# GpSimd takes over the high halves of the FFN weights, and three of the FFN's waits move

## The reference

```
def _tlin(x, w, s):                       # w holds -1, 0 and 1
    return jnp.einsum('bsi,oi->bso', x, w) * s
h = jax.nn.silu(_tlin(x, w1_w, w1_s)) * _tlin(x, w2_w, w2_s)      # 512 -> 2048
h = jax.nn.gelu(_tlin(h, h1_w, h1_s), approximate=False)          # 2048 -> 2048
h = jax.nn.gelu(_tlin(h, h2_w, h2_s), approximate=False)          # 2048 -> 2048
return _tlin(h, w3_w, w3_s)                                       # 2048 -> 512
...
x = x + jnp.tanh(g_xattn[0]) * _L0_xattn_ref(_layernorm(x), ctx_1024, ...)
x = x + jnp.tanh(g_ffn[0]) * _L0_ffn_ref(_layernorm(x), ...)      # this one
x = x + jnp.tanh(g_xattn[1]) * _L1_xattn_ref(_layernorm(x), ctx_1024, ...)
x = x + jnp.tanh(g_ffn[1]) * _L1_ffn_ref(_layernorm(x), ...)
```

## Time and profile before

| | before |
|---|---|
| median of 3 runs (1685.14 to 1689.29) | 1686.5 us |
| the profiled execution, its own time | 1688.01 us |
| its span in the trace | 1686.2 us |
| PE busy | 1601.1 us, 95% of the span |
| DVE, ACT, POOL busy | 1100.2, 966.3, 290.8 us |
| FFN of layer 0 (first to last start of L995) | 520.4 to 1074.1 us |

### The profile page before, as it was taken

How to read it: one execution, slowest core, us unless ns; L and a number is a source line. 1 busy time by engine, 2 the same in 40 slices (tenths; PEclk the granted TensorE clock), 3 DMA queues, 4 the chain that set the end, 5 groups by cost and what they waited for, 6 DMA issues and landing times.

```text
span 1686.2 us, 25732 instructions
## 1 busy us (share of the span) xinstructions
PE 1601.1 (95%) x9298; PEld 1448.8 (86%) x9298; DVE 1100.2 (65%) x1949; ACT 966.3 (57%) x2014; POOL 290.8 (17%) x407
## 2 busy tenths in 40 slices
PE   5899999999988999999899989989999999999898
PEld 5788999899977999999899986777999989998655
DVE  5367877787786673333655545546777777778786
ACT  4367776777664454343544444236767667776575
POOL 2022121212142000000100000002111111113641
PEclk9999999999999999999999999999999999999899
DMA  6567776776562225554255625354766577657400
GB/s 191 129 157 180 189 180 167 179 190 178 144 179 78 90 89 185 189 175 170 94 197 203 215 98 169 106 122 122 194 169 178 151 186 183 167 137 191 155 12 28
DMA packets 146232, 257.74 MB, mean 153 GB/s; under 512 B 40916, under 2 KB 90196, under 8 KB 145968
## 3 DMA queue, kind: packets, MB, share of 16 engines
q1 hardware_dynamic: 145648, 255.79, 54.1%
q10 hardware_dynamic: 448, 0.14, 0.0%
HBM read 187.46 MB, written 58.57 MB: 146 GB/s over the span
## 4 chain that ended last, share of the span: by engine, by line
PE 82%; DVE 6%; issue 5%; ACT 4%; DMA 1%; POOL 1%; ACTq 0%; SPq 0%; DVEq 0%; POOLq 0%
PE ps L995 26%; PE ps L684 16%; PE ps L680 14%; PE ps L731 7%; PE ps L743 7%; PE ps L801 2%; PE ps L718 2%; PE ps L721 2%; PE ps L936 2%; PE ps L949 1%; ACT P L1654 1%; DVE wl_f L1546 1%; PE ps L859 1%; PE ps L720 1%; PE ps L719 1%
## 5 line engine op out<-in xcount | busy, mean ns | idle before, releaser
L995 PE MATMUL ps<-ah_f,wh_f 128*128 128x400 f32 (+1 forms) x1296 | 446.5, 346 | 9.3 <-DVE al_f L1559 5.6
L995 PE MATMUL ps<-al_f,wh_f 128*128 128x400 f32 (+1 forms) x1296 | 444.7, 344 | 0.0
L995 PEld LDWEIGHTS ps<-ah_f,wh_f 128*128 128x128 f32 x1296 | 245.4, 189 | 12.5 <-issue 10.7
L995 PEld LDWEIGHTS ps<-al_f,wh_f 128*128 128x128 f32 x1296 | 245.7, 190 | 0.0
L1154 DVE TENSOR_REDUCE nmax<-ps 100x1 f32<-100x722 f32 x256 | 220.6, 903 | 38.3 <-PE ps L720 34.7
L1654 ACT ACTIVATE P<-ps,nmax 100x722 f32<-100x722 f32 x256 | 220.2, 862 | 32.2 <-DVE nmax L1154 32.1
L1983 POOL TENSOR_TENSOR cxl<-raw,cxh 128x384 fp32r<-128x384 f32 (+1 forms) x120 | 118.9, 1013 | 659.9 <-ACT cxh L1619 653.0
L1663 ACT ACTIVATE PT<-ps 128x400 fp32r<-128x400 f32 x384 | 166.9, 505 | 80.1 <-PE ps L731 78.9
L1160 DVE TENSOR_TENSOR PT<-ps,PT 128x400 fp32r<-128x400 f32 x384 | 196.7, 566 | 3.6
L680 PE MATMUL ps<-cxh,wkh 128*128 128x338 f32 (+1 forms) x512 | 174.7, 341 | 22.9 <-DVE wkl L1133 13.3
L1542 DVE CAST wh_f<-raw_f 128x1024 fp32r<-128x1024 f32 x85 | 58.8, 691 | 184.8 <-PE ps L995 160.5
(11 more groups left out here) (191 smaller groups left out, 2614.9 us busy)
## 6 DMA issues: line engine op xcount, KB each, us to landing
KS<-kd SPq DMA_DIRECT2D x192, 361.0 KB
raw_f<-in_h SPq DMA_DIRECT2D x64, 512.0 KB, 5.0
raw_f<-in_gud SPq DMA_DIRECT2D x48, 512.0 KB, 5.8
raw<-in_ctx SPq DMA_DIRECT2D x64, 192.0 KB, 3.6
kd<-ksh SPq DMA_DIRECT2D x64, 192.0 KB, 2.1
kd<-ksl SPq DMA_DIRECT2D x64, 192.0 KB, 2.4
raw_f<-in_w SPq DMA_DIRECT2D x24, 512.0 KB, 3.8
raw<-in_ctx SPq DMA_DIRECT2D x64, 169.0 KB, 4.5
```

The costliest lines, as they stand in the source:

```text
L995: return e.matmul(o, p, q, start=start, stop=stop)
```

## The change

GpSimd casts unit u's high half (`high_unit`, new semaphore g_wh), for units 3 to 87. DVE keeps the subtraction, which now waits for g_wh, and makes it at the start of step u instead of its end; ACT's measure moves to the start of its step too. Steps 47 and 79 (`LATE`) keep both at the end. PE waits for g_wh ahead of a unit, and for g_low only at the load of the register. Unit 16 takes k = 4 to 7 before 0 to 3. The products of unit 80 begin after 62 Gelus instead of 64 and wait for 64 at batch 6, whose bank the last Gelu reads.

```diff
+LATE = (47, 79)
...
             def high(z, jobs):
                 for j in jobs:
+                    if j[3] and j[2][1] == 6 * S:
+                        w.wait_ge(a_gelu, 64)
                     one((wh, act[0]), z, j, j[4], False)
...
                 if u < 3:
                     w.wait_ge(g_ul, u + 1)
                 else:
-                    w.wait_ge(v_ul, u - 2)
+                    w.wait_ge(g_wh, u - 2)
+                for k, jobs in groups[:-1]:
+                    input_ready(u, k)
+                    high(z, jobs)
+                input_ready(u, groups[-1][0])
                 if u < 3:
                     w.wait_ge(v_low, 1)
                 else:
                     w.wait_ge(g_low, u - 2)
-                for k, jobs in groups[:-1]:
-                    input_ready(u, k)
-                    high(z, jobs)
-                input_ready(u, groups[-1][0])
                 e.reg_load(reg, low[0:1, z, 1:2].bitcast(I32))
...
+                order = [4, 5, 6, 7, 0, 1, 2, 3] if u == 16 else range(8)
...
-            w.wait_ge(a_gelu, 64)
+            w.wait_ge(a_gelu, 62)
...
-            def prepare(u):
+            def low_unit(u):
+
                 z, r = u % 4, FETCHED["unit", u] % 4
-                w.wait_ge(d_raw[r], raw_done(("unit", u)))
+                w.wait_ge(g_wh, u - 2)
                 if u >= 4:
                     w.wait_ge(p_u, u - 3)
-                me.then(e.tensor_copy(wh[:, z, :], raw[:, r, :]))
-                me.settle()
-                if u >= 4:
                     w.wait_ge(a_raw, FREE_AT["unit", u - 4] + 1)
...
             for u in range(UNITS):
+                if u + 3 < UNITS and u not in LATE:
+                    low_unit(u + 3)
...
-                if u + 3 < UNITS:
-                    prepare(u + 3)
+                if u in LATE:
+                    low_unit(u + 3)
...
             for u in range(UNITS):
+                if u + 3 < UNITS and u not in LATE:
+                    measure_low(u + 3)
...
-                if u + 3 < UNITS:
+                if u in LATE:
                     measure_low(u + 3)
...
+            def high_unit(u):
+
+                z, r = u % 4, FETCHED["unit", u] % 4
+                w.wait_ge(d_raw[r], raw_done(("unit", u)))
+                if u >= 4:
+                    w.wait_ge(p_u, u - 3)
+                e.tensor_copy(wh[:, z, :], raw[:, r, :]).then_inc(g_wh, 1)
+
             attention(0)
+            high_unit(3)
             for u in range(UNITS):
+                if 4 <= u + 1 < UNITS:
+                    high_unit(u + 1)
                 if u >= 3:
                     spread_low(u)
```

More of the change, by code:

```diff
@@ L281, in flamingo_kernel @@
         g_ones, g_cx, g_ql, g_rx, g_low, g_tot = (sem("g_" + n) for n in ("ones", "cx", "ql", "rx", "low", "tot"))
-        g_xf, g_ul = (sem("g_" + n) for n in ("xf", "ul"))
+        g_xf, g_ul, g_wh = (sem("g_" + n) for n in ("xf", "ul", "wh"))
         g_self, g_nh, g_xr, g_wo, g_ol, g_rq, g_xn, g_xq = (
@@ L1058, in _ @@
                         w.wait_ge(a_gelu, 32 * layer + 2 * (n - 4) + 2)
+                order = [4, 5, 6, 7, 0, 1, 2, 3] if u == 16 else range(8)
                 products(u, [(8 * q + kk, [(ps[:, p + half, 0:HN], (128 * kk, 128 * kk + 128),
                                             (8 * q + kk, HN * half, HN * half + HN), False,
-                                            q == 0 and kk == 0, q == 1 and kk == 7) for half in range(2)])
-                             for kk in range(8)]).then_inc(p_u, 1)
-            w.wait_ge(a_gelu, 64)
+                                            q == 0 and i == 0, q == 1 and i == 7) for half in range(2)])
+                             for i, kk in enumerate(order)]).then_inc(p_u, 1)
+            w.wait_ge(a_gelu, 62)
             for u in range(80, 88):
```

## The result

The changed kernel takes 1660.7 us, median of four runs (1659.97 to 1663.37), against 1685.8 for the kernel before on the same chip: a ratio of 0.985 with a 95% interval of 0.983 to 0.987. The time is 1.5% lower, and the interval lies clear of 1. The forecast was 1663.0, faster, with a range of 1660 to 1670. The profiled execution took 1663.37 us (span 1661.6) against 1688.01 (span 1686.2).

The account below looks back on a forecast made before the run. PE, busy 95% of the span, was taken to bound the kernel, losing time at three layer boundaries. Gains 3.6 + 10.2 + 9.4 + 0.3 = 23.5 us from 1688.0 give 1664.5, less 1.5 for the median: 1663.0, range 1660 to 1670.

Parts of the forecast that it names:

- three boundaries: Layer boundaries 15/16, 47/48 and 79/80 in the FFN, where PE stands still and the clock falls behind it.
- Unit 16: Boundary 15/16: starting with k = 4 to 7 covers DVE's late splits; 7.2 us instead of 10.78, gain 3.6.
- Boundary 47/48: Unit 49's measure and subtraction ahead of the copies: units 49 and 50 without waits, 11.66 us instead of 21.86, gain 10.2.
- GpSimd waits out DVE's streams: Shared memory: GpSimd's casts yield to DVE's back-to-back work; if one came between two splits, unit 49 would lose 0.8 us.
- Unit 80: Boundary 79/80: starting after 62 Gelus leaves no wait; 7.37 us instead of 16.81, gain 9.4.
- The first wait: Start of the FFN: PE's wait on v_low moves behind 12 matmuls, gain 0.3 us.
- Casts on GpSimd cost nothing: Every step: 85 casts of 1.04 us join the all-reduces, 1.4 us in every 5.83, hidden by PE's products.
- The reload: GpSimd's library reload at the start, behind unit 4's cast: margin 0.7 us; costs nothing at 6.96 us, 2.1 at 9.76.
- the late all-reduce: Rival at unit 50: all-reduce late behind unit 51's cast, most of the 10.2 us lost, 1673; chance 4%.
- the wait at the register load: Rival: the wait keeps PE from running ahead, up to 0.5 us in each of 88 units, 1707; chance 4%.
- a reload in each unit: Rival: GpSimd reloads its library between cast and all-reduce, some 215 us slower, 1880; chance 2%.
- given back in part: Rival: long reload (2.1), cast inside the splits (0.8), clock falling at unit 16 (1.5); together 4.4 us, 1667.4; chance 13%.

Follow-up runs that it names:

- experiment 10: The kernel before, unchanged, run again for a second trace: 1685.9 us, ratio 1.000.
- experiment 8: Changed kernel with GpSimd's first cast held, unit 16 in order 4, 5, 6, 0, 1, 2, 3, 7, and unit 51's cast held past the splits: 1660.5 us.
- Experiments 4 and 6: First: kernel before with only unit 80's early start, 1683.1 us. Second: changed kernel without exceptions at steps 47 and 79 (LATE empty), 1676.9 us.
- experiment 7: Changed kernel with PE's wait for g_low back at the head of a unit: 1666.5 us, ratio 0.989.
- experiment 12: Changed kernel with every cast of a high half made twice on GpSimd: 1669.6 us, ratio 0.990.
- Experiment 5: Changed kernel with the casts of the high halves given back to DVE, everything else still moved: 1659.3 us, ratio 0.984.
- (3): Kernel before with only the casts of the high halves moved to GpSimd: 1681.5 us, ratio 0.997.
- experiments 2: Changed kernel with GpSimd's first cast held until DVE's last normalization of attention is made: 1659.3 us, ratio 0.984.
- the padded kernel: Changed kernel with first cast held and an unused second BATCH_NORM_STATS2 on DVE ahead of the last normalization: 1661.7 us, ratio 0.987.

## Why the prediction was right

The time was forecast from waits at three boundaries, and these waits are gone but for 0.8 us. Two things were not forecast, a loss at the start and a gain outside the FFN. In the first trace they largely cancel, 5.4 against 7.4 us, and that is luck. Nor is the agreement at the boundaries as close as it looks. The terms were read from one trace of the kernel before and are compared with that same trace here. In its second trace (experiment 10) the three windows sum to 47.04 us instead of 49.45, so against that one the same change gives 20.2 us, not 22.6.

**Unit 16: 3.6 forecast, 3.53 measured.** k = 0 starts 0.2 us late, k = 1 to 3 follow DVE's pace, and 0.50 us stand ahead of the register load (0.6 forecast). The clock stayed at 1.00, as I had costed it, and in the traces of all changed kernels. The 3.53 contain a fall of the clock in the first trace of the kernel before; against the second they are 2.3.

**Boundary 47/48: 10.2 forecast, 9.65 measured.** The mechanism is as told: the Gelu 47 right behind the copies, unit 49 without a wait ahead of it, and the all-reduce of unit 50 off the path. The term was 0.55 us too large, because GpSimd's cast of unit 51 did come in between two splits (809.09); experiment 8 holds that cast back, and unit 49 takes 5.83 us instead of 6.39. So here the step that failed is "GpSimd waits out DVE's streams": the row of 5757 ns from which it came showed only that GpSimd can be kept waiting. In the changed kernel GpSimd's first cast, issued 0.09 us ahead of DVE's normalization, made it last 1.22 us instead of 0.55. The cast at 809.09 was held up by 0.43 us (1.47 less 1.04) while a split ran, and then held up the next split (2.73 us for the two instead of 1.88). The exclusive lock that the Trainium skill describes (SBUF — State Buffer, "Who interferes with whom": who issues first has the shared ports for the whole instruction) agrees with the order in both, and with the times of the second. The first is shorter than a full block would make it: 0.95 us to the cast's end and 0.55 behind it are 1.50, and 1.22 were measured. With a cast among the splits the prediction's sum was 22.7, of which 22.4 at the three boundaries, against 22.6.

**Unit 80: 9.4 forecast, 9.44 measured.** Experiments 4 and 6 show that the two edits there need each other: the early start alone gives 2.8, and without the exception at step 79 some 5.5 are lost again.

**The first wait, 0.3:** gone, as forecast; experiment 7 brings it back (0.33).

**Casts on GpSimd cost nothing:** true of the even stretches, even doubled (12), but not of the start (0.7 us) and of 47/48 (0.55). Experiment 5 shows that they also gain nothing beside the moved measures. Alone they gave 5 us (3): they shorten the same queue on DVE that the moved measures empty. Gains that work on one queue do not add.

**The reload:** costed at nothing, and it cost nothing. Its uncovered time was 5.57 us, where I had taken 6.96. In the trace of the changed kernel PE itself came late, which hid it further, but in experiments 2 and 8 PE was on time (15.94 and 15.96 us for units 0 and 1), the reload took 5.87 and 5.98 us, and there is no gap at units 3 to 5 either. In experiment 12, with two more casts ahead of it and PE late again, it cost nothing too.

**Not in the prediction: the start.** I looked at the first cast only as something ahead of the reload, not at who was using the memory just then. The collision costs 0.7 us in every trace with the first cast unheld (eight of 14 traces have the 2.1 us wait, seven of them by the cast). In five of these seven the clock fell right behind it, which cost 3.2 to 5.2 us more (19.78 to 21.80 against 16.60; 0.4 of the highest belong to an earlier fall), and in none of the six traces with a wait of 1.43 to 1.46. Holding the cast gave a median 6.6 us lower than the changed kernel's beside it. That the collision is there and that holding the cast removes it is shown; that the length of the wait alone makes the fall likely is not, since the padded kernel's one trace had none, and a wait of 3.04 us at unit 16 (experiment 10) had none either. What else decides is open.

**Not in the prediction: outside the FFN.** Ahead of the FFN the 2.3 us are chance: the changed kernel's own three traces lie 4.4 us apart there. The stretch behind the FFN took 612.1 and 611.8 us in the kernel before and 610.1 and 610.6 with one edit alone, 606.6 to 608.6 in nine traces of changed kernels, and 610.4 with the casts doubled. None of the edits touches it. Part is a wait that some traces have and others not (ACT for the transfer of `ksl`, 1.75 us, PE 0.9; experiment 10 says in which), part the clock's falls in it. Why these go with the kernel is open; they are worth 3 to 5 us of the measured gain. The forecast of 23.5 us thus met 25.1, 20.7 and 20.7 in three measurements. In the first trace it was 22.6 gained at the boundaries, 5.4 lost at the start and 7.4 gained outside.

Of the rivals, the late all-reduce, the wait at the register load (experiment 7: units of 5.83 either way) and a reload in each unit did not occur. Of "given back in part" one of three parts came true, the cast inside the splits.

## What to carry to other kernels

Where an in-order engine's queue holds work for later (a measure, a subtraction) ahead of work that is wanted now, changing the order is worth more than moving the work to another engine: here the new order gave as much without the second engine as with it (experiment 5), and the second engine alone a fifth of it (experiment 3). When GpSimd gets a new large instruction, look at which DVE instruction it meets at each place where it may first start, since 1 us of it can hold up a DVE instruction on the critical path; one wait placed on DVE's result takes that away. And count what the clock does behind a wait into the price of the wait, as a chance: here 2.1 us cost 0.7 more than 1.45 did, or 4 to 6 more. And take a second trace of the kernel before ahead of a sum: the three stretches took 49.45 us in one and 47.04 in the other, with the same waits.

## What the runs showed of the hardware

GpSimd's cast of 128 x 1024 from 32 bits, issued 0.09 us ahead of DVE's TENSOR_SCALAR of 100 x 512, made that one last 1.22 us instead of 0.55. The other way round, a cast issued 0.07 us behind a DVE subtraction of 1.22 us took 2.05 us instead of 1.04, in the timeline of the changed kernel behind unit 16.

```profile
628.39 1.22 DVE L1552 TENSOR_TENSOR wl_f<-raw_f,wh_f 128x1024 fp32r<-128x1024 f32 x1
628.46 2.05 POOL L2175 CAST wh_f<-raw_f 128x1024 fp32r<-128x1024 f32 x1 [5.89 <-PE ps L999]
```

Casts and all-reduces took turns on GpSimd 85 times with one reload, whose uncovered time was 5.57 to 5.98 us in the ten traces with casts right ahead of it, and 6.77 in the kernel with the casts on DVE:

```profile
534.54 0.38 POOL L2170 PARTITION_ALL_REDUCE low_f<-low_f  x1 [6.77 <-issue]
```

A wait of PE of 2.1 us was followed by half clock in five traces and not in three, with the same matmuls around it; one of 3.05 us was followed by it in one trace of the kernel before, and one of 3.04 at the same place was not in the other.
